# First projection's term stores and weight column order, and where the windowed attention applies its queries' norms

## The reference, cut to what matters

```python
q, k, v = split(x @ wqkv)
q = l2norm(q) * q_scale ; k = l2norm(k) * k_scale     # per row and head
q, k = rotary_xpos(q), rotary_xpos(k)
p = softmax(8 * q k^T + window/causal mask)           # 128-token windows
y = (p @ v) @ wo
```

## Time and profile before

| | |
|---|---|
| median of three runs | 6057.34 us |
| the profiled execution | 6057.39 us, its span 6055.7 us |
| TensorE's mean granted clock | 0.873 of full speed |
| `qkv` of stage 0 | about 18 to 221 us of the span |
| `relative_attention` | about 222 to 905 us |
| `rotary_qkv`, two layers | about 3138 to 3408, 4026 to 4293 us |
| `windowed_attention`, two layers | about 3408 to 3750, 4293 to 4660 us |

### The profile page before, as it was taken

The page is one execution under the profiler, slowest core; times in us unless marked ns, Lnnn a source line. Parts: engine busy times, 40 slices in busy tenths (PEclk is TensorE's granted clock), DMA queues, the critical chain, the costliest instruction groups (busy, mean ns, idle before and its releaser), DMA issues. The chain is left out here.

```text
span 6055.7 us, 94426 instructions
## 1 busy us (share of the span) xinstructions
PE 4584.0 (76%) x24898; PEld 2861.8 (47%) x24898; DVE 3893.7 (64%) x8139; ACT 2858.2 (47%) x6148; POOL 2021.5 (33%) x3169
## 2 busy tenths in 40 slices
PE   6577773928789748996757677887676977995897
PEld 3244432417433327872336455776455853334434
DVE  5566666386388764443779766569766556885566
ACT  1366662143257633234545456335465324773353
POOL 0244430000176412223435542225541215542342
PEclk8798996969889879997779889999898998997897
DMA  5788871000533202104522321012321035323533
GB/s 176 252 304 307 306 250 53 0 0 0 184 100 93 76 12 78 43 25 127 154 78 106 119 81 37 22 40 106 117 81 35 7 109 149 88 72 102 171 117 103
DMA packets 326728, 648.04 MB, mean 107 GB/s; under 512 B 72914, under 2 KB 140148, under 8 KB 326345
## 3 DMA queue, kind: packets, MB, share of 16 engines
q1 hardware_dynamic: 259256, 463.30, 23.2%
q0 software_dynamic: 67104, 180.70, 10.3%
HBM read 361.41 MB, written 251.28 MB: 101 GB/s over the span
## 5 line engine op out<-in xcount | busy, mean ns | idle before, releaser
L813 DVE TENSOR_REDUCE t_nmax<-t_aps 128x2 f32<-128x1024 f32 x700 | 837.7, 1222 | 278.0 <-PE t_aps L735 272.6
L920 ACT ACTIVATE t_expT<-t_bps 128x512 f32<-128x512 f32 x1290 | 701.5, 599 | 283.2 <-PE t_bps L754 234.5
L754 PE MATMUL t_bps<-t_Q,t_K 51*128 51x512 f32 (+2 forms) x1290 | 524.7, 468 | 61.3 <-ACT t_expT L920 43.0
L735 PE MATMUL t_aps<-t_K,t_Q 49*128 49x512 f32 (+2 forms) x1400 | 463.1, 459 | 63.8 <-DMA t_K<-k_halves 28.7
L754 PEld LDWEIGHTS t_bps<-t_Q,t_K 51*128 51x128 f32 (+2 forms) x1290 | 228.0, 189 | 528.6 <-ACT t_expT L920 372.1
L2097 DVE TENSOR_TENSOR f_hl<-f_h,f_hh 128x512 fp32r<-128x512 f32 x192 | 203.7, 1061 | 411.4 <-ACT f_hh L2022 411.4
L781 PE MATMUL t_ops<-t_expT,t_V 128*17 128x512 f32 (+1 forms) x2560 | 413.8, 614 | 0.4 <-ACT t_expT L920 0.4
L3514 ACT ACTIVATE t_relsb<-t_relsb,t_nmax 128x128 f32<-128x128 f32 (+3 forms) x512 | 288.7, 564 | 220.0 <-DVE t_nmax L3486 219.5
L2386 POOL TENSOR_TENSOR a_crossed<-a_qsb,a_tab 128x256 f32<-128x256 f32 x272 | 266.3, 1000 | 294.0 <-ACT a_qsb L2333 263.0
L3392 POOL TENSOR_TENSOR t_relsb<-t_relsb,t_M 128x128 f32<-128x128 f32 x512 | 216.6, 454 | 387.7 <-DMA t_relsb<-rel 387.7
L854 POOL DMA_DIRECT2D t_Q<-q_halves x525 | 270.9, 518 | 147.3 <-POOLq L78 73.8
(11 more groups left out here) (439 smaller groups left out, 12455.8 us busy)
## 6 DMA issues: line engine op xcount, KB each, us to landing
rel<-t_rows SPq DMA_DIRECT2D x128, 640.0 KB, 4.4
t_relsb<-rel SPq DMA_DIRECT2D x128, 640.0 KB, 6.3
t_Q<-q_halves POOLq DMA_DIRECT2D x420, 64.0 KB, 2.5
t_K<-k_halves POOLq DMA_DIRECT2D x420, 64.0 KB, 2.6
k_halves<-a_parts SPq DMA_DIRECT2D x48, 512.0 KB, 4.8
q_halves<-a_parts SPq DMA_DIRECT2D x48, 512.0 KB, 5.6
o_xT<-attended SPq DMA_DIRECT2D x32, 512.0 KB
f_R<-combine SPq DMA_DIRECT2D x128, 128.0 KB, 2.9
```

Source lines behind the costliest of these rows:

```text
L735: last = nc.tensor.matmul(aps[:, (t * PPG + i) % 2, x, :], operand(Qr, KA, p, h, slice(t * P, (t + 1) * P)), operand(Kr, KA, p, h, slice(0 ...
L754: nc.tensor.matmul(bps[:, slot_of(kb, j), :], operand(Kr, KB, p, h, slice(kb * P, (kb + 1) * P)), operand(Qr, KB, p, h, slice(0, S)), star ...
L813: nc.vector.tensor_reduce(nmax[:, g, t, i * HPT:(i + 1) * HPT], aps[:, (t * PPG + i) % 2], AX.X, ALU.max, negate=True).then_inc(s["maxed"], 1)
L920: nc.scalar.activation(expT[:, kb % RING, j, :], bps[:, slot_of(kb, j), :], ACT.Exp).then_inc(s["expo"], 1 + (PAD if end else 0))
```

## The change

Stage 0: the weight columns and the biases are put into the order dimension, head (4 copies on VectorE, two small bias transfers more), so that the terms lie in DRAM as `[6 terms, 256, tokens]`. `TERMS` is put into an order in which the query terms are parts 1, 2, 3, 1, 2, 1 and the key terms 1, 1, 1, 2, 2, 3. A job is then stored in three transfers, of three, two and one terms, and every job of a batch has a part buffer of its own.

Stage 5: `rn` lives outside both functions. Only the key units are multiplied by it in `rotary_qkv`; the query units are transposed as they come from `turned`. In `windowed_attention` the queries' norm is the scale of the exponential, and one small VectorE instruction a unit makes its bias from the maximum and the norm. Signs of tables and masks follow.

```diff
-TERMS = ((1, 1), (1, 2), (2, 1), (1, 3), (3, 1), (2, 2))
+TERMS = ((1, 1), (2, 1), (3, 1), (1, 2), (2, 2), (1, 3))
...
-        parts = sb("parts", [P, 2, 3, S], BF16)
+        parts = sb("parts", [P, nj, 3, S], BF16)
...
+                    if k in biases:
+                        for c in range(KT):
+                            x = view[0:1, 0:1]
+                            by_dim = bass.AP(x.tensor, x.offset + c * (P // DH) * KT, [[1, DH], [DH * KT, P // DH], [1, 1]])
+                            sp.dma_start(W[k][:, c:c + 1], by_dim, allow_slow_non_contiguous=True).then_inc(s["w"], 16)
...
-                        h = row // 16
-                        for i, term in enumerate(TERMS):
-                            part = term[dst is not qdst] - 1
-                            sp.dma_start(dst[h:h + P // 16, i * 16:(i + 1) * 16, ds(b * S, S)], parts[:, j % 2, part]).then_inc(s[f"parts_st{j % 2}"], 16)
+                        for first, many, part in ((0, 3, 0), (3, 2, 1), (5, 1, 2)):
+                            terms = parts[:, j, 0:many] if dst is qdst else parts[:, j, part:part + 1].broadcast_to([P, many, S])
+                            sp.dma_start(dst.rearrange("r f t -> f r t")[row:row + P, first:first + many, ds(b * S, S)], terms).then_inc(s[f"parts_st{j}"], 16)
...
-                        dve.wait_ge(s[f"parts_st{j % 2}"], b * (ST * k) + ST * (j // 2) + 16)
+                        dve.wait_ge(s[f"parts_st{j}"], b * ST + 16)
...
                 rows(0, 0, 0)
+                dve.wait_ge(s["w"], 16 * NW)
+                for k in turned:
+                    for c in range(KT):
+                        nc.vector.tensor_copy(Wt[k][:, c, :].rearrange("p (d h) -> p h d", d=DH),
+                                              W[k][:, c, :].rearrange("p (h d) -> p h d", d=DH)).then_inc(s["wt"], 1)
...
-                pe.wait_ge(s["w"], 16 * len(weights))
+                pe.wait_ge(s["w"], 16 * NW)
+                pe.wait_ge(s["wt"], KT * len(turned))
...
-        straight = sb("straight", [P, 4, HD])
+        straight = sb("straight", [P, NU, HD])
-        rot = sb("rot", [P, 2, HD])
+        rot = sb("rot", [P, HD])
...
-                        pe.wait_ge(s["scaled"], n + 1 + 4)
+                        if u % 2:
+                            pe.wait_ge(s["scaled"], b * NT + u // 2 + 1 + NT)
+                        else:
+                            pe.wait_ge(s["rot"], n + 1 + 2)
                         alone(pe)
                         pe.wait_ge(s["turned"], n + 1)
+                        x = rot if u % 2 else straight[:, u, :]
...
-                    dve.wait_ge(s["scaled"], n + 1)
-                    nc.vector.tensor_tensor(heads(straight[:, u % 4, :]), heads(qsb[:, i, :]),
+                    if i:
+                        dve.wait_ge(s["scaled"], b * NT + t + 1)
+                    else:
+                        dve.wait_ge(s["tp"], n + 1)
+                    alone(dve)
+                    nc.vector.tensor_tensor(heads(straight[:, u, :]), heads(qsb[:, i, :]),
...
-                    if i and at(1):
-                        scaled(at(1))
+                    if i and at(2):
                         scaled(at(2))
...
+                    if i == 0:
+                        act.wait_ge(s["bias"], u.n + 1)
                     for x in range(2):
-                        act.wait_ge(s["least"], u.n * 4 + i * 2 + x + 1 + 4)
-                        nc.scalar.activation(prob[:, u.slot, i, x, 0:w], summed[:, u.slot, i, x, 0:w], ACT.Exp, scale=-1.0,
+                        h = u.j * 2 + x
+                        nc.scalar.activation(prob[:, u.slot, i, x, 0:w], summed[:, u.slot, i, x, 0:w], ACT.Exp,
+                                             scale=rn[:, ds(u.b * NT + t, 1), h:h + 1].rearrange("p o h -> p (o h)"),
                                              bias=nmax[:, u.slot, i, x:x + 1], accum_out=esum[:, u.slot, i, x:x + 1]).then_inc(s["expo"], 1)
...
-                                                           scale=1.0, scalar=3.0e38, op0=ALU.add, op1=ALU.min,
-                                                           accum_out=nmax[:, u.slot, i, x:x + 1]).then_inc(s["least"], 1)
+                                                           scale=1.0, scalar=-3.0e38, op0=ALU.add, op1=ALU.max,
+                                                           accum_out=top[:, u.slot, i, x:x + 1]).then_inc(s["least"], 1)
+
+                def bias(u):
+                    dve.wait_ge(s["least"], u.n * 4 + 4 + 4)
+                    nc.vector.scalar_tensor_tensor(nmax[:, u.slot], top[:, u.slot], -1.0, rn[:, ds(u.b * NT + u.half * 2, 2), u.j * 2:u.j * 2 + 2],
+                                                   ALU.mult, ALU.mult).then_inc(s["bias"], 1)
...
                 def step(at):
+                    if at(6):
+                        bias(at(6))
                     if at(5):
                         inverse(at(5))
...
-                        pool.dma_start(dst[:, p, h:h + H // QH, :], src.rearrange("h r t -> r h t")[:, h:h + H // QH, b * S:(b + 1) * S]).then_inc(s[f"{what}{p}"], 16)
+                        pool.dma_start(dst[:, p, h:h + H // QH, :], src.rearrange("r (d h) t -> (r d) h t", h=H)[:, h:h + H // QH, b * S:(b + 1) * S]).then_inc(s[f"{what}{p}"], 16)
...
-        qs = dram("q_terms", [16, 96, TOK], BF16)
-        ks = dram("k_terms", [16, 96, TOK], BF16)
+        qs = dram("q_terms", [6, D, TOK], BF16)
+        ks = dram("k_terms", [6, D, TOK], BF16)
```

More of the change, by code:

```diff
@@ L145, in qkv @@
     nj = len(jobs)
-    ST = 16 * len(TERMS)
+    ST = 16 * 3
+    DH = 16
+    biases = sorted({j[3] for j in jobs})
+    NW = len(weights) + len(biases) * (KT - 1)
+    turned = sorted({j[0] for j in jobs})
     scaled = sorted({(j[3], j[4]) for j in jobs if j[3] and j[4] != 1.0})
     with phase(nc, name, "w c0 c1 c_free stats rstd xn xn_free xt_ps xt_ps_free xt xt_free "
-               "job job_free q32 q32_free parts parts_st0 parts_st1 v v_free v_sb v_st0 v_st1 dvc poolc actc") as (s, sb, ps):
+               "job job_free q32 q32_free parts parts_st0 parts_st1 parts_st2 parts_st3 wt v v_free v_sb v_st0 v_st1 dvc poolc actc") as (s, sb, ps):
         W = {k: sb(k, shape) for k, (view, shape) in weights.items()}
+        Wt = {k: sb(f"{k}_turned", weights[k][1]) for k in turned}
         xn = sb("xn", [P, 2, NT, D])
@@ L173, in _ @@
             def _(sp):
-                for c in ("parts_st0", "parts_st1", "v_st0", "v_st1"):
+                for c in ("parts_st0", "parts_st1", "parts_st2", "parts_st3", "v_st0", "v_st1"):
                     sp.sem_inc(s[c], 16)
                 for k, (view, shape) in weights.items():
-                    sp.dma_start(W[k][tuple(slice(None) for _ in shape)], view).then_inc(s["w"], 16)
+                    if k in biases:
[4 more added lines that the diff above has]
+                    else:
+                        sp.dma_start(W[k][tuple(slice(None) for _ in shape)], view).then_inc(s["w"], 16)
                 def load(b, p):
@@ L207, in _ @@
                     save(NB - 2 + p, p)
-                sp.wait_ge(s["parts_st0"], 16 + ST * NB * ((nj + 1) // 2))
-                sp.wait_ge(s["parts_st1"], 16 + ST * NB * (nj // 2))
+                for j in range(nj):
+                    sp.wait_ge(s[f"parts_st{j}"], 16 + ST * NB)
                 for p in range(2):
@@ L349, in _ @@
                             pe.wait_ge(s["job_free"], b * nj + j + 1)
-                            o, w, x = jps[:, j % 4, :], W[wn], source(sc)
+                            o, w, x = jps[:, j % 4, :], Wt[wn], source(sc)
                             if tile_k:
@@ L2413, in _ @@
                         x = tab[:, 2 * i + j]
-                        last = nc.vector.scalar_tensor_tensor(x, x, 1.0 if i else -1.0, sc[:, i, j, :].unsqueeze(1).broadcast_to([P, NT, DH]), ALU.mult, ALU.mult)
+                        last = nc.vector.tensor_tensor(x, x, sc[:, i, j, :].unsqueeze(1).broadcast_to([P, NT, DH]), ALU.mult)
                 last.then_inc(s["tab"], 1)
@@ L2421, in norms @@
                     t = u // 2
-                    return (b * NT + t, *(x[:, t % 2, :] for x in (ss, held, root, inv, bend, rn)))
+                    return (b * NT + t, *(x[:, t % 2, :] for x in (ss, held, root, inv, bend)), rn[:, ds(b * NT + t, 1), :].rearrange("p o h -> p (o h)"))
                 def limit(at):
@@ L2454, in turned @@
                     dve.wait_ge(s["crossed"], n + 1 + 2)
-                    nc.vector.tensor_tensor(straight[:, u % 4, :], straight[:, u % 4, :], crossed[:, i, :], ALU.add).then_inc(s["rot"], 1)
+                    nc.vector.tensor_tensor(straight[:, u, :], straight[:, u, :], crossed[:, i, :], ALU.add).then_inc(s["rot"], 1)
                 def scaled(at):
@@ L2463, in scaled @@
                     alone(dve)
-                    dve.wait_ge(s["tp"], n + 1)
-                    nc.vector.tensor_tensor(heads(rot[:, i, :]), heads(straight[:, u % 4, :]),
```

(9 more changed lines are left out.)

36 lines of the change are left out of this document (19 added, 17 removed).

## The result

The kernel after takes **5965.93 us**, the median of four runs (5963.57 to 5978.32), beside 6060.77 us for the kernel before (6056.36 to 6085.98, four runs). The recorded ratio is 0.9833, with a 95% interval of 0.981 to 0.9855; the two medians alone give 0.9844. The profiled execution is the one of 5963.57 us, its span 5961.9 us, TensorE's mean granted clock 0.885. Forecast were 5977 us, with a range of 5925 to 6025.

What follows compares the result with a forecast made beforehand. It took half-used DMA engines on stage 0's stores, VectorE in the rotary stage and a dependency chain in the windowed attention as bounds. -52 - 48 + 20 = -80 us on 6057.4 gave 5977 us, range 5925 to 6025.

Steps and rivals of the forecast that it cites:

- Stage 0: Stage 0's projection: wide stores use all 16 DMA engines, VectorE then bounds a 17.3 us batch; -52 us, ends 0 and -65.
- the late start: Start of stage 0: two more bias issues and four reorder copies make TensorE start 2.5 us later.
- The buffers: Stage 0: with four part buffers a split waits for stores a whole batch old, costed at nothing.
- 0 if the rate stays at 160 GB/s: Stage 0's lower end: no gain if the term stores keep their old rate.
- rival A: Stage 0: the stores gain nothing, their rate stays 160 GB/s; 6029 us in total, chance 0.09.
- Relative attention: Attention behind stage 0: changed distance between loaded pieces in DRAM costs 0, ends -4 and +8 us.
- Rotary: Rotary stage: one 128x512 multiplication a tile removed from VectorE, 64 in both layers; -48 us, ends -30 and -75.
- Rival B: Rotary stage finds another bound after 0.3 us a tile, 19 us in place of 48; 6006 us, chance 0.12.
- VectorE is the bound: Rotary stage: VectorE, busy 233.8 of 242 us, sets the pace; a tile falls from 7.5 to 6.7 us.
- Windowed: Windowed attention: longer exponentials cost 17 us, the bias instruction some 0.05 us a pair; +20 us, ends 0 and +60.
- Rival D: Windowed attention: bias joins every unit's chain and all four exponentials are longer, +129 us; 6086 us in total, chance 0.04.
- Rival C: Nothing is paid in the windowed attention and stage 0 overlaps better; 5944 us, chance 0.13.

Runs made afterwards that it cites:

- six_stores: Kernel after with each stage 0 term stored by itself, six wide stores a job in place of three; 5967.53 us, stage 0 ends at 169.0 us.
- eight_outer: Kernel of six_stores with DRAM rows padded so a store's outermost dimension is 8; 5997.22 us, stage 0 ends at 203.6 us.
- extra_mul: Kernel after with one more 128x512 multiplication a rotary tile, of a query unit by its norms into an unread buffer; 6022.44 us.
- no_bias: Kernel after with the raw maxima as the exponential's bias, without the bias instruction and its wait; 5954.26 us.
- four_buffers_only: Kernel before with four part buffers and the old stores; 6065.63 us, stage 0 ends at 203.4 us.

## Why the prediction was right

Forecast -80 us, measured -93.8 us between the two profiles and -94.8 between the medians (6060.77 and 5965.93); the time is 11 us under the point, inside the range. By the terms:

- **Stage 0: -52 forecast, -52.3 measured.** The end was to be at 169 us and is at 168.7, the batch 17.3 us and is 17.5 to 17.9, the late start 2.5 us and is 2.0. The eight splits take 130.6 us (32.2 to 162.8) against 129.6 forecast. That half of the engines was used was read from a share of 0.54, and the pair six_stores and eight_outer bears it out (34.6 us). One step of it was wrong beside the right sum. The buffers were costed at nothing, with the remark that with slow stores the old wait comes back; alone they give 17.6 us, because the queue was not full before. So the lower end too was wrong, "0 if the rate stays at 160 GB/s", and so was rival A's 6029 us: at that rate a gain of 17.6 us would have been left. With the buffers first, the wide stores are worth 34.7 of the 52 us and not all of it. The rate itself was right: 320 to 340 GB/s were assumed, and the slices show 310 to 360 at nine tenths while transfers run. The 240 GB/s at 0.71 are the mean with the pauses that VectorE's pace leaves.
- **Relative attention: 0 forecast, +0.6 measured.** The other distance between pieces costs nothing: the loads land in 5.9 and 6.0 us, against 6.1.
- **Rotary: -48 forecast, -46.2 in this pair, -48.8 by the means.** 0.76 us a tile against 0.8 taken, between the 0.67 of the shortest instruction and the 0.917 of the mean. The reason given, that part of the long instruction is GpSimd's and stays, is borne out: `a_held` grew from 266 ns to 561 when the multiplication left, and is 166 without GpSimd's work. The sum came out in part by luck: 64 x 0.8 us was some 3 us too much (extra_mul shows 24.2 us a layer, 48.4 in both), and the 3 us taken off for `rn` addressed by a register don't show, since the multiplication alone gives back all but 0.2 of the 24.4 us a layer. `a_held` in the kernel before (groups, 3200 to 3380 us):

```profile
L2427 DVE TENSOR_SCALAR a_held<-a_ss 128x16 f32<-128x16 f32 x24 | 6.4, 266 | 0.0
```

  Strictly by the port rule 43 us were to be saved; 48.8 are, more than its bare length. Rival B (another bound after 0.3 us a tile) is out: VectorE is still busy for 127.25 of 130 us. But "VectorE is the bound" was too coarse, since a reduction of 0.67 us in the same place costs a quarter of the multiplication.
- **Windowed: +20 forecast, +8.5 in this pair, +5.4 by the means.** This is the term that was mis-sized, and the largest miss of the sum: 11.5 of the 13.8 us between forecast and profiles. The step that failed is that the added work was taken to lengthen the stage by itself, with no term for TensorE's clock. The work came as read: exponentials of 598 ns as with two operands, and a bias instruction of 299 ns. At equal TensorE time the two are estimated above at 9.6 us a layer, 19 in both, which is the +20. But the same matmuls took 8.8 us less of TensorE a layer (261.2 against 270.0 us by the means), which at 0.78 gives some 7 us back. Within the 19 us the split looks different from the forecast's 17 for the exponentials and 3 for the bias instruction, rather 15 and 8, with the uncertainty given there. The waits fit: VectorE's inverse waits 24.3 us for the exponentials, against 30.1 before, since the bias instruction now stands ahead of it; in no_bias it waits 39.9 (170 us each). Why the clock rose stays open. Rival D (the bias on every unit's chain) is out: the exponentials waited twice in 170 us, 2.9 us together. Rival C (nothing paid here, stage 0 overlapping better) is nearest in this stage's measured time, but by the estimate not for its reason, and stage 0 did not overlap better; the time (5966) lies between its 5944 and the forecast's 5977.
- The rest of the difference, -4.5 us, lies in stages that neither kernel changes, and the forecast has no part in it.

## What to carry to other kernels

A DMA share that stays flat near a half while an engine waits for stores deserves a look at the outermost dimension of both patterns: 128 rather than 8 there was worth 35 to 46 us here, and twice as many issues nothing. Read the share in short slices, since a mean mixes the rate with the pauses. Don't price a VectorE instruction beside a busy GpSimd by its bare length or by VectorE's busy share: part of the recorded time is waiting, which moves to the next instruction. In one place here a reduction of 0.67 us cost 0.20 us a tile and a multiplication of the same bare length 0.76. Extra buffers are worth most while the transfers are slow (17.6 us) and least once they are fast (6.4 us), so cost the parts of a change in both orders. And before a stage of one kernel is compared with that of another, compare TensorE's busy time for the same matmuls in both.

## What had not been expected of the hardware

**An untouched stage moves with the clock.** The projection `a7` near the end (the stage that the rows below cover) is the same code in all kernels and does the same work. Its stretch, from its first weight load to its barrier, before, in four_buffers_only, and after:

```profile
5543.00:5663.00 120.00, 97.09 (x464) 73.13 (x464) 58.73 (x145) 34.30 (x50) 10.12 (x16) 0.81 0.50 184
```

```profile
5530.00:5669.00 139.00, 116.39 (x464) 87.07 (x464) 58.77 (x144) 34.34 (x50) 10.36 (x18) 0.68 0.44 159
```

```profile
5450.00:5570.00 120.00, 97.08 (x464) 73.13 (x464) 58.61 (x145) 34.27 (x50) 10.12 (x16) 0.81 0.51 184
```

The same 464 matmuls take 116.39 us of TensorE in place of 97.09, at a granted clock of 0.68 in place of 0.81; VectorE's and ScalarE's work is unchanged. These 19 us are as much as the four buffers had gained 5300 us earlier. Why the clock was granted otherwise there isn't shown. A total of one execution can therefore hide or invent a gain of 0.3%, and the stage has to be read.

**Stage 0 also got a faster TensorE.** Its granted clock rose from 0.80 to 0.97; its busy time fell from 136.08 to 122.97 us for the same 384 matmuls. The forecast had no such term. It went by 15 us of TensorE a batch; at the old 136.08 us for eight batches it would have been 17.0, hardly below VectorE's 17.3. What the stage would take at the old clock no run shows.
